# Half of a gate tile ahead of a barrier, and eleven weight low parts from GpSimd to VectorE, in an attention and FFN kernel

## What is computed

```python
x = hidden_states                                     # (4, 512, 512), fp32
x = x + _L0_attn_ref(_layernorm(x), w_attn, b_attn, w_proj, b_proj)
...
INTER = 1376
gate = jax.nn.silu(jnp.einsum('bsh,ih->bsi', x, w_gate))      # x here: _layernorm(x)
up = jnp.einsum('bsh,ih->bsi', x, w_up)
x = x + jnp.einsum('bsi,hi->bsh', gate * up, w_down)
```

## Time and profile before

| what | us |
|---|---|
| median of 3 runs | 850.94 (850.01 to 852.06) |
| the profiled execution's own time | 846.56 |
| its span, first to last instruction | 844.8 |
| TensorE busy | 791.0 |
| VectorE busy | 649.4 |
| ScalarE busy | 414.8 |
| GpSimd busy | 312.2 |

### The profile page before, as it was taken

One profiled execution on the slowest core, in us unless ns is written; L12 is line 12 of the kernel. 1 busy time (PEld: TensorE's weight loads), 2 busy tenths in 40 slices (PEclk: granted clock), 3 DMA queues, 4 the chain that ended last, 5 costly groups with the idle time before them and its releaser, 6 DMA issues. The chain is left out here.

```text
span 844.8 us, 13420 instructions
## 1 busy us (share of the span) xinstructions
PE 791.0 (94%) x4554; PEld 546.2 (65%) x4554; DVE 649.4 (77%) x1598; ACT 414.8 (49%) x796; POOL 312.2 (37%) x446
## 2 busy tenths in 40 slices
PE   3899799999999999999998889999999899999998
PEld 3655455556555565556554578888877678888886
DVE  6498787878887888877886256759998788888773
ACT  4335656655656556565666524333436234334441
POOL 5213333342443434423433404324434434433342
PEclk9999999999999999999999999999999999999999
DMA  8773656546574575747662425042115322221052
GB/s 279 202 248 106 181 170 202 184 145 212 165 240 139 167 214 166 241 124 218 207 184 92 167 86 185 26 149 75 39 62 175 111 83 94 75 76 50 13 171 90
DMA packets 76332, 122.80 MB, mean 145 GB/s; under 512 B 14035, under 2 KB 39302, under 8 KB 76265
## 3 DMA queue, kind: packets, MB, share of 16 engines
q1 hardware_dynamic: 74217, 121.69, 45.4%
q10 hardware_dynamic: 2048, 0.27, 0.2%
HBM read 79.34 MB, written 42.32 MB: 144 GB/s over the span
## 5 line engine op out<-in xcount | busy, mean ns | idle before, releaser
L748 ACT ACTIVATE pt<-bank 128x512 f32<-128x512 f32 (+1 forms) x384 | 193.4, 529 | 130.6 <-PE bank L1183 117.9
L919 DVE CUSTOM_DVE_ANT_0 bank<-bank,mask_qk 128x512 f32<-128x512 f32 (+3 forms) x416 | 195.9, 512 | 47.7 <-PE bank L1158 45.8
L1183 PE MATMUL bank<-q_st,k_st 116*128 116x512 bf16 (+3 forms) x512 | 132.8, 302 | 16.5 <-ACT pt L748 15.0
L1158 PE MATMUL bank<-k_st,q_st 97*128 97x512 bf16 (+3 forms) x512 | 132.6, 306 | 5.8 <-DMA q_st<-slopes_dram 4.1
L1508 POOL TENSOR_TENSOR wd_lo<-wd_raw,wd_hi 128x512 fp32r<-128x512 f32 x44 | 59.9, 1370 | 152.4 <-ACT wd_hi L1537 152.4
L653 POOL TENSOR_SCALAR_AFFINE_SELECT pt<-pt 128x256 f32<-128x256 f32 x128 | 56.1, 438 | 129.1 <-ACT pt L748 129.1
L1158 PEld LDWEIGHTS bank<-k_st,q_st 97*128 97x128 bf16 x512 | 42.0, 98 | 67.7 <-issue 38.9
L657 POOL TENSOR_SCALAR_AFFINE_SELECT pt<-pt 128x256 f32<-128x256 f32 x128 | 53.2, 416 | 74.9 <-ACT pt L748 74.7
L1200 PE MATMUL bank<-pt,v_nat 128*32 128x512 f32 (+3 forms) x1024 | 76.6, 440 | 3.0 <-POOL pt L653 2.3
L1896 PE MATMUL bank<-wd_hi,w_hi 128*128 128x512 f32 x176 | 70.6, 401 | 6.1 <-issue 3.0
L1183 PEld LDWEIGHTS bank<-q_st,k_st 116*128 116x128 bf16 x512 | 44.6, 98 | 48.2 <-ACT pt L748 24.1
(11 more groups left out here) (184 smaller groups left out, 1719.1 us busy)
## 6 DMA issues: line engine op xcount, KB each, us to landing
stack_dram<-scratch SPq DMA_DIRECT2D x32, 384.0 KB, 3.1
q_st<-stack_dram SPq DMA_DIRECT2D x32, 384.0 KB
k_st<-stack_dram SPq DMA_DIRECT2D x32, 384.0 KB
wd_raw<-w_down SPq DMA_DIRECT2D x44, 256.0 KB, 3.5
xt<-w_gate_up SPq DMA_DIRECT2D x20, 512.0 KB, 3.5
stack_dram<-scratch SPq DMA_DIRECT2D x32, 256.0 KB, 3.6
pv_dram<-weighed SPq DMA_DIRECT2D x32, 256.0 KB, 4.4
weighed<-pv_dram SPq DMA_DIRECT2D x17, 256.0 KB
```

The lines of the kernel that those rows point to most:

```text
L748: act.activation(pt[:, h % PT_RING, COL0[k]:COL0[k] + WIDE[k]], bank[3 + (3 * h + k) % 2][:, 0:WIDE[k]], ACT.Exp, scale=1.0 / HD).then_inc ...
L919: last = dve.tensor_tensor_reduce(bank[k][:, at:at + n], bank[k][:, at:at + n], mask_qk[:, S - n:S], 1.0, NEG, ALU.add, ALU.max, mx[:, h % ...
L1158: last = pe.matmul(bank[k][:, at:at + n], q_st[0:K_MAX, s, h % 4, t * P:(t + 1) * P], k_st[0:K_MAX, s, h % 4, 0:n], start=True, stop=not b ...
L1183: last = pe.matmul(bank[3 + u % 2][:, at:at + n], k_st[0:K_EXP, s, h % 4, t * P:(t + 1) * P], q_st[0:K_EXP, s, h % 4, t * P:S], start=True ...
```

## The change

It has two parts. The first: the gate product of plain tile 3 of batch 0 (12 matmuls into bank 4) moves from the FFN block into the attention block, behind the last projection block; a new semaphore `half_made` tells the FFN block that it is there, and `tile(0)` skips it. It waits for `gu_done`, the third gated product, whose bank it overwrites.

The second: `down_lo(11)` to `down_lo(21)`, which GpSimd made after the last unit of the first pair, are now made by VectorE, number 11 behind the low part of the last even product, and each other one ahead of its tile's `product_lo`. GpSimd goes straight on to the weight sums of the next unit; at the first unit of the second pair it waits until VectorE's low parts are counted.

```diff
@@ -1258,6 +1259,10 @@
             gate_up(1)
             gate_up(2)
             project_block(3)
+            pe.wait_ge(gu_done, AHEAD_TILES)
+            f = AHEAD_TILES
+            exact_product(pe, bank[4], [(wgu_e_hi[:, f, 0, k, :], wgu_e_lo[:, f, 0, k, :], fT_hi[:, k, :], fT_lo[:, k, :])
+                                        for k in range(KT)]).then_inc(half_made, 1)
 
 
 def qk_split_count():
@@ -1279,7 +1284,7 @@
 
 
 def ffn(nc, tokens_dram, wgu_d, wd_d, out_d, bank, ident, minus_half, hT_hi, hT_lo, wgu_early, early_in, x1_stored,
-        wgu_e_hi, wgu_e_lo, gu_hi, gu_lo, w_hi, w_lo):
+        half_made, wgu_e_hi, wgu_e_lo, gu_hi, gu_lo, w_hi, w_lo):
 
 
     out_v = out_d.rearrange("b (t p) d -> b t p d", p=P)
@@ -1524,8 +1529,9 @@
                 if u in BEHIND:
                     down_lo(BEHIND[u] + 1)
                 if u == FIRST:
+                    pool.wait_ge(wd_lo_done, PAIR)
                     down_lo(PAIR)
-                if u in END:
+                if u == len(UNITS) - 1:
                     for n in range(END[u], END[u] + FT):
                         down_lo(n)
 
@@ -1680,6 +1686,14 @@
                     dve.wait_ge(gu_lo_done, i)
                 dst, done = (gu_even[:, :], even_done) if b == 0 else (gu_odd[:, f, :], odd_done)
                 dve.tensor_tensor(dst, bank[5 + 2 * (i % 2)][:, :], gates[:, i % 2, :], ALU.mult).then_inc(done, 1)
+
+            def down_lo(n):
+
+                if n == FT:
+                    dve.wait_ge(wd_lo_done, FT)
+                dve.wait_ge(wd_hi_done, n + 1)
+                dve.tensor_tensor(wd_lo[:, n % WD, :], wd_raw[:, n % RAW_DOWN, :], wd_hi[:, n % WD, :].bitcast(F32),
+                                  ALU.subtract).then_inc(wd_lo_done, 1)
 
             def product_lo(n):
                 b, f = DOWNS[n]
@@ -1824,8 +1838,12 @@
                 dve.wait_ge(summed, 7 * u + 7)
                 dve.tensor_tensor(gu_even[:, :], u2, gates[:, 0, :], ALU.mult).then_inc(even_done, 1)
                 product_lo(DOWNS.index((2 * pair, f)))
+                if u == FIRST - 1:
+                    down_lo(FT)
                 if u in END:
                     for i in range(FT - 1):
+                        if u == FIRST - 1:
+                            down_lo(END[u] + 1 + i)
                         product_lo(END[u] + 1 + i)
                         if i == 0:
                             add_residual(2 * pair)
@@ -1851,6 +1869,10 @@
                 if i >= EVEN_TILES + 2:
                     released(pe, i - 2)
                 for c in range(2):
+                    if (i, c) == (0, 0):
+                        pe.wait_ge(half_made, 1)
+                        pe.sem_inc(tile_done, 1)
+                        continue
                     if (b, f) == (0, EARLY):
                         pe.wait_ge(plain_lo_done, c + 1)
                     exact_product(pe, bank[4 + 2 * (i % 2) + c],
```

More of the change, by code:

```diff
@@ L237, in kernel_body @@
         x1_stored = [whole.enter_context(nc.semaphore(f"x1_stored{i}")) for i in range(2)]
+        half_made = whole.enter_context(nc.semaphore("half_made"))
         tokens_dram = nc.dram_tensor("tokens_dram", [B, TT, P, D], F32, kind="Internal").ap()
         attention(nc, x_d, wqkv_d, bqkv_d, wproj_d, bproj_d, qx_d, kx_d, tokens_dram, bank, ident, minus_half, fT_hi, fT_lo,
[L241 removed]
+                  xt, wgu_d, wgu_early, early_in, x1_stored, half_made, w_hi, w_lo, wgu_e_hi, wgu_e_lo, gu_hi, gu_lo)
         ffn(nc, tokens_dram, wgu_d, wd_d, out_d, bank, ident, minus_half, fT_hi, fT_lo, wgu_early, early_in,
[L243 removed]
+            x1_stored, half_made, wgu_e_hi, wgu_e_lo, gu_hi, gu_lo, w_hi, w_lo)
 def attention(nc, x_d, wqkv_d, bqkv_d, wproj_d, bproj_d, qx_d, kx_d, tokens_dram, bank, ident, minus_half, fT_hi, fT_lo,
[L247 removed]
+              xt, wgu_d, wgu_early, early_in, x1_stored, half_made, w_hi, w_lo, wgu_e_hi, wgu_e_lo, gu_hi, gu_lo):
     x_v = x_d.rearrange("b (t p) d -> b t p d", p=P)
```

3 lines of the change are left out of this document (removed).

## The result

| what | before | changed |
|---|---|---|
| median, us | 850.79 (846.84 to 852.06, 9 runs) | 844.60 (839.96 to 845.93, 9 runs) |
| ratio to before | | 0.9937, 95% interval 0.9915 to 0.9959 |
| the profiled execution's own time | 846.56 | 842.5 |
| its span | 844.8 | 840.8 |

What follows compares the result with a forecast made beforehand. TensorE was taken as the bound, busy 791.0 of 844.8 us, with VectorE holding most of the chain between the pairs. Part 1 at 0.0 and part 2 at -1.2 gave 849.7 us, range 847.6 to 852.1.

Steps and rivals of the forecast that it cites:

- the case chosen: Whole kernel: a slow clock stretch in both old and new kernel, or in neither; 0.0 - 1.2 = -1.2 us, chance 0.38.
- Part 1, the barrier: Barrier between the program's halves: TensorE arrives later with 12 matmuls moved ahead, release 0.6 us late, at most 0.96.
- Part 1, the transposes: Second batch's transposes: they wait for normalised tokens, whose chain starts 0.6 later; start at 520.4 against 520.41, worth 0.0.
- Step a): Last even product's down tile, first pair: number 11 (+0.6) and GpSimd's weight sums (+1.0) start it 1.6 us late, at 634.8.
- Step b): Two rounds of combinations between the pairs: each gives back 0.5 us; number 18's down tile starts at 659.1, 1.1 late.
- Step c): From number 18's tile to the next unit: TensorE no longer waits 2.08 us or runs slowly; end 670.7 instead of 673.46.
- The slow stretch cost 1.6: Behind the 2.08 us wait: 36 matmuls at the lower clock took 10.02 us and would take 8.2 at full clock.
- -1.2 remains if the clock is taken out: Low parts on VectorE, between the pairs: -2.8 us in all, -1.2 without the slow stretch, bounds -1.7 to -0.7.
- Rival 1: Whole kernel: the waits cure the clock, a slow stretch in the old kernel only; 0.0 - 2.8, 848.1 us, chance 0.22.
- rival 4: Barrier not late, so tokens early: -0.6 - 1.2, or with the clock -3.4; 849.1 to 847.5 us, chance 0.09.
- Rivals 2 and 3: Late tokens and slow clock before the transposes, 851.7 to 853.3, chance 0.16; moves cancel between the pairs, 850.7, chance 0.15.
- The signs named: Release about 504.4, down tile at 634.8, VectorE low parts 0.6 to 0.7; wrong if transposes before 519.8 or after 520.8.

Runs made afterwards that it cites:

- the filled barrier: Kernel before with the 12 gate-half matmuls done twice, ahead of the barrier (result thrown away) and behind it as before; 845.96 us, ratio 0.9977.
- the kernel with the wait filled: Kernel before with six matmuls, result thrown away, in TensorE's 2.08 us wait before the third last down tile of the first pair; 844.45 us, one time.
- the gate half alone: Changed kernel with all down low parts given back to GpSimd, the gate half still ahead of the barrier; 848.91 us, ratio 0.9997 to the kernel before.

## Why the prediction was wrong

**The size.** Forecast -1.2 us, range +1.2 to -3.3 around 850.9. In the stretch that the change touches it was -3.95. The times fit that: the 21 executions of the changed kernel, nine of the first comparison and twelve later, have a mean of 843.5, the 48 later ones of the kernel before and the 8 of its copy one of 847.4, 3.9 apart. Of the 5.4 us of the first comparison some 1.5 are thus scatter; and the 850.94 on which I put the forecast was itself 3.5 above the later mean, so the us of the forecast were bound to come out high. That is no step of the working. From -1.2 to -3.95 it is 2.75, and the steps below account for it: 1.6 by the case chosen, 1.0 by number 11, 0.3 by the transposes, and 0.1 back between the pairs and by rounding.

**Part 1, the barrier: right.** Release 0.63 later for 0.6 forecast; the filled barrier had 0.46.

**Part 1, the transposes: 0.0 forecast, 0.33 gained, 0.1 to 0.8 in all profiles.** "All of it starts 0.6 later" failed. What the normalisations wait for is not the statistics, which were done at 510.91, but GpSimd's low parts, and these wait for ScalarE's cast of a down weight and so for that weight's load; the earlier trace rows already names ScalarE as what released them. The chain of waits of the changed kernel has it:

```profile
505.96 4.76 DMA wd_raw<-w_down
...
510.74 0.63 ACT wd_hi L1543
...
511.44 2.54 POOL wd_lo L1513 x2
...
514.77 1.06 POOL rstd L199
```

Counted from the last projection matmul, GpSimd's first low part starts at 10.74 (10.42 before) and the normalisations end at 19.00 (18.81 before): 0.2 late where I had 0.6. In all fourteen profiles that low part starts 0.70 behind the start of ScalarE's cast, and with the gate half ahead and GpSimd's order unchanged it starts anywhere from 10.34 to 11.08, by when the load lands; in four profiles without the gate half ahead it is 10.06 to 10.42. The mean of the first seven is 0.5 later, the barrier's 0.6 nearly, and their normalisations end 0.3 later. What makes the load land early or late was not tried; from 506 to 514 the DMA share is 1.00 before and 0.98 in the changed kernel, so a load shares the DMA engines with others there. In these seven profiles the transposes started 18.62 to 19.31 behind the anchor, 0.4 earlier on average than the 19.36 to 19.39 of before. (The forecast's 520.41 was the start of a merged piece; in the timeline the first transpose of before starts at 520.25.)

**Step a): right in what it counted, blind in front.** +1.57 for 1.6, and of it +1.06 from the weight sums (1.0) and +0.5 from number 11 (0.6). But I wrote that GpSimd's 11 low parts lie between the pairs and summed from 628.1 on. Number 11 lay in the unit before, behind number 10, and there it stretched a weight low part of VectorE from 0.41 to 1.51. This is the step of the working that failed: its saving of 1.0 to 1.1 us was put at nothing, and giving number 11 back shows it. By the rule that I used myself (operations with both inputs in SBUF and GpSimd take turns) each of the 11 removed operations had to be looked up with its neighbours; number 11 wasn't.

**Step b): right.** From the last even tile to number 18 it is 24.42 us, forecast 659.1 - 634.8 = 24.3.

**Step c): the time right, its split wrong.** The end piece is 3.9 us shorter, as forecast (15.48 to 11.57). "The slow stretch cost 1.6" and "-1.2 remains if the clock is taken out" is what failed: filling the wait took the clock's loss away and gave 0.83. Against the kernel with the wait filled, which has no slow matmuls, the change still wins 3.1 in this piece (14.65 to 11.57); my own sum would have had to keep 2.0, not 1.2.

**The case chosen: the largest miss.** Both sums were written down, and the smaller was made the forecast: "a slow stretch is as likely there as it was at 501 and 661". That took back 1.6 of the 2.8, more than any other step was off. The runs say otherwise. The clock fell behind the wait of 2.08 in each of the four profiles that have it unfilled in the program of before or with the gate half alone; it didn't in any of the four with the barrier's 2.56, nor behind the 1.8 to 2.0 in front of the last even tile in the five profiles that have one. One profile can't tell a habit from an accident; but the same profile had 2.56 without a fall, so idle time by itself was no ground to expect one elsewhere. Rival 1, at 848.1 and with 0.22, had the mechanism between the pairs; rival 4's -3.4 came nearest to the stretch's -3.95, by its number and not by its reason.

**Rivals 2 and 3** didn't come true. No slow stretch stands in front of the transposes (their wait is 1.23; 1.6 to 2.1 was forecast), and TensorE waits 0.19 for number 18 and not at all behind it. The rule that the prediction named from the Trainium skill (Perfetto Trace Analysis, "Optimizing Scalar/DVE Operations"), that a saturated VectorE give work away, to GpSimd if need be, is not borne out here: taken by itself it meant a loss of some 6.6 us, and the page of the changed kernel has VectorE busy for 3.1 us less. The doubt that the skill adds, for the port that the two share, is.

**Luck.** The end piece came out 3.9 shorter, as forecast, though half of what the forecast put down to the clock was VectorE's lateness: both went together.

**The signs named.** The release (504.28 for 504.4) and VectorE's low parts of 0.7 came, and no wait stood ahead of the last three down tiles. The down tile of the last even product started at 633.36 and not at 634.8, and the transposes at 519.76, just past the sign of being wrong (519.8).

## What to carry to other kernels

Before an instruction is taken away from an engine that shares something with another, list every neighbour of each single instance, those outside the place that the edit is about as well: one of eleven paid a quarter of the gain here. Where an engine's operations run at 2.6 times their usual length beside another engine, moving work **to** the slowed engine can shorten its queue. And where a slow clock and a late producer stand at one place, the two don't add: fill the wait and see what is left.

## What the runs showed of the hardware

- VectorE's operations with both inputs in SBUF last 0.68 alone, 1.2 beside GpSimd's 128x256 sums and 1.78 beside its 128x512 low parts, three in a row; one with an input in PSUM kept its 0.68 in the midst of the sums (629.34). The Trainium skill (SBUF — State Buffer, "Who interferes with whom") says that a VectorE instruction with two SBUF inputs contends with a GpSimd instruction that reads SBUF, and that one with at most one SBUF input doesn't, outside the modes that use two ports for one input. The trace agrees with both halves.
- The four normalisations, each with one large input, took 3.85 us beside two GpSimd low parts and 4.90 beside three; in the last unit of the first pair three of them lasted 1.44, that is 0.48 each, with GpSimd idle for all but the end. By these numbers each low part costs them 1.0 us. So one large SBUF input did not protect them; no run shows in which mode they ran.
- TensorE's clock fell to its lower level behind a wait of 2.08 us, in four of four profiles (six to eight matmuls start 0.43 us apart there and not 0.23), and did not behind one of 2.56 elsewhere, in none of four; six matmuls of 0.23 each inside the 2.08 kept it up. What else distinguishes the two places was not tried.
- Ahead of 490 us, in code that is the same in all kernels, the clock fell at places that differ from execution to execution, and the last projection matmul started anywhere from 497.4 to 506.4. A copy of the kernel before measured 0.5% under it. An execution's mean granted clock goes with its time: 1.5 us longer for each 0.002 less, over 57 executions of one program.
